# k's layout for the scores: rows laid by 0/1 matmuls in place of copies through DRAM, with q and k turned together on VectorE

## The reference, cut to what matters

```python
# x: [1, 4096, 256], 16 heads of 16, float32
q = (x @ Wq.T + bq).reshape(B, S, H, hd).transpose(0, 2, 1, 3)
k = (x @ Wk.T + bk).reshape(B, S, H, hd).transpose(0, 2, 1, 3)
v = (x @ Wv.T + bv).reshape(B, S, H, hd).transpose(0, 2, 1, 3)
q, k = _apply_rope(q, cos, sin), _apply_rope(k, cos, sin)   # (xr, xi) -> (xr c - xi s, xr s + xi c)
scores = softmax(einsum('bhqd,bhkd->bhqk', q, k) / sqrt(256))
x = _layernorm(x + (scores @ v -> [B, S, D]) @ Wo.T)
x = _layernorm(x + ffn(x))    # gated, two gelu layers of 1024, out to 256
```

## Time and profile before

| | before |
|---|---|
| three runs | 3526.78 us (median), 3524.37 to 3530.44 |
| the profiled execution | 3524.76 us, its span 3523.1 us |
| TensorE busy / weight loads | 3384.9 us (96%) / 1536.3 us |
| VectorE busy | 2987.0 us (85%) |
| ScalarE busy | 2451.1 us (70%) |
| Pool busy | 184.7 us (5%) |
| mean granted clock of TensorE | 0.971 |

### The profile page before, as it was taken

How to read it: one execution, slowest core, us unless ns; L and a number is a source line. 1 busy time by engine, 2 the same in 40 slices (tenths; PEclk the granted TensorE clock), 3 DMA queues, 4 the chain that set the end, 5 groups by cost and what they waited for, 6 DMA issues and landing times. The chain is left out here.

```text
span 3523.1 us, 67331 instructions
## 1 busy us (share of the span) xinstructions
PE 3384.9 (96%) x27994; PEld 1536.3 (44%) x27994; DVE 2987.0 (85%) x3188; ACT 2451.1 (70%) x4472; POOL 184.7 (5%) x320
## 2 busy tenths in 40 slices
PE   8569999999999999999999999999999699999998
PEld 3223333333333333333333333333333278888887
DVE  6599999999999999999999999999996045555554
ACT  2108888888888888888888888888889622222222
POOL 3300000000000000000000000000000000000000
PEclk9759999999999999999999999999999899999999
DMA  8920000000000010001000000000000220000000
GB/s 212 219 42 6 20 12 12 24 12 12 12 24 16 15 60 14 12 11 61 11 12 30 14 12 12 12 12 12 12 8 5 92 96 25 25 25 26 25 13 13
DMA packets 60037, 113.78 MB, mean 32 GB/s; under 512 B 11719, under 2 KB 23624, under 8 KB 59560
## 3 DMA queue, kind: packets, MB, share of 16 engines
q1 hardware_dynamic: 53048, 93.83, 9.7%
q0 software_dynamic: 6688, 15.68, 1.5%
HBM read 82.20 MB, written 37.22 MB: 34 GB/s over the span
## 5 line engine op out<-in xcount | busy, mean ns | idle before, releaser
L710 DVE TENSOR_REDUCE group_max<-wide 128x2 f32<-128x1024 f32 x2048 | 2473.0, 1223 | 22.5 <-PE wide L521 15.8
L681 ACT ACTIVATE probs<-scores 128x512 f32<-128x512 f32 x4046 | 2202.9, 600 | 290.1 <-PE scores L606 42.0
L547 PE MATMUL sums<-probs,v_all 128*17 128x256 f32 (+1 forms) x16120 | 1277.2, 389 | 7.7 <-ACT mixed L664 6.8
L606 PE MATMUL scores<-q_sb,k_all 51*128 51x512 f32 x3968 | 988.5, 495 | 6.7 <-ACT probs L681 5.7
L521 PE MATMUL wide<-k_all,q_sb 48*128 48x512 f32 x4096 | 850.1, 411 | 52.9 <-DVE group_max L710 26.7
L606 PEld LDWEIGHTS scores<-q_sb,k_all 51*128 51x128 f32 x3968 | 370.6, 183 | 842.9 <-ACT probs L681 829.4
L547 PEld LDWEIGHTS sums<-probs,v_all 128*17 128x17 f32 x16120 | 267.1, 95 | 747.4 <-issue 364.9
L521 PEld LDWEIGHTS wide<-k_all,q_sb 48*128 48x128 f32 x4096 | 397.6, 190 | 91.5 <-DVE group_max L710 63.9
L1073 ACT ACTIVATE whole_hid<-acc,scale 128x512 f32<-128x512 f32 x128 | 84.7, 689 | 297.5 <-PE acc L954 297.3
L954 PE MATMUL acc<-hid_b,h2T 128*128 128x512 f32 x1024 | 241.6, 397 | 0.0
L954 PE MATMUL acc<-hid_a,h1T 128*128 128x512 f32 x1024 | 240.2, 394 | 0.0
(11 more groups left out here) (88 smaller groups left out, 1171.1 us busy)
## 6 DMA issues: line engine op xcount, KB each, us to landing
k_all<-k_parts SPq DMA_DIRECT2D x96, 128.0 KB, 5.2
q_sb<-q_parts SPq DMA_DIRECT2D x192, 64.0 KB, 2.5
q_parts<-parts SPq DMA_DIRECT2D x16, 512.0 KB, 6.0
k_parts<-parts SPq DMA_DIRECT2D x16, 512.0 KB, 6.3
heads<-mixed SPq DMA_DIRECT2D x128, 34.0 KB
xt<-in_xT SPq DMA_DIRECT2D x8, 512.0 KB, 6.3
w_words<-in_h1T POOLq DMA_DIRECT2D x32, 128.0 KB, 2.4
w_words<-in_h2T POOLq DMA_DIRECT2D x32, 128.0 KB, 2.3
```

Source lines behind the costliest of these rows:

```text
L547: last = pe.matmul(sums[32 * j:32 * j + HD + 1, cols], v_all[:, g, kt, j], probs[(kt * HG + j) % RING][:, cols], start=(kt == 0 and cols.s ...
L606: pe.matmul(scores[(s + e) % BANKS][:], k_all[rows, g * GP + j, n // HG * P:(n // HG + 1) * P], q_sb[g][rows, j], start=True, stop=True).t ...
L681: act.activation(probs[n % RING][:], bank, ACT.Exp, scale=INV_SCALE)\
L710: dve.reduce_max(group_max[:, n], wide[n % 2][:], AX_X).then_inc(wide_free, 1)
```

## The change

k is not stored in DRAM any more. q and k of one half of features form one item of 1024 columns, so there are 16 items in place of 32: VectorE's shuffle, multiplications, addition, rounding and subtraction each take both together, and VectorE multiplies by the sines too. For k's part of an item, TensorE runs eight matmuls in fp32r (`spread_k`): on each of four row tiles of 32 rows (two heads) a 0/1 matrix picks the high part for its two places in both halves, and a second one the low part for its place, summed into one bank per row tile. ScalarE copies the four banks into `k_all`, adding a column that is 1 in the rows of ones and 0 elsewhere. q's and k's projections have one bank each, in place of four in turn; the order of the work on TensorE is written out: q and k of the first half, v, the spread of the previous chunk's second half, q and k of the second half, the spread of the first half. v's bias is added by one fp32r matmul over all rows (bias high part in one row, low part in another) in place of the float32 one of a single row. `v_all` has its token tiles outermost, so ScalarE copies two tiles of v at once. One of the two `parts` buffers lies in the last columns of `k_all`, which are written last. The loops are written out rather than run as hardware loops. In `attend` the last placement, the rows of ones and the waits for them are gone. The core of the diff:

```diff
-def place_k(sp, k_parts, k_all, c, ft, done):
...
@@ project @@
...
+        item = [sb(f"item{b}", [P, 2, CH]) for b in range(2)]
+        pair = sb("pair", [P, 2, CH])
+        lent = k_all[:, JP:, (NCH - 1) * CH:].rearrange("p (a t) s -> p a t s", a=2)
+        parts = [lent, sb("parts", [P, 2, 2, CH], F32R)[:]]
...
+        ps = [psum(f"ps_{t}", [P, CH]) for t in "qk"]
...
+        spread = [psum(f"ps_spread{j}", [P, CH]) for j in range(JP)]
...
-                place_k(sp, parts_dram[1], k_all, c, ft, k_in)
...
+            for c in range(NCH):
+                for ft in range(FT):
+                    i = c * FT + ft
+                    sp.wait_ge(low_done, i + 1)
+                    dst = q_dram.rearrange("a f s -> f a s")[ft * P:(ft + 1) * P]
+                    sp.dma_start(dst[:, :, c * CH:(c + 1) * CH], parts[i % 2][:, :, 0].bitcast(F32)).then_inc(q_stored[i % 2], 16)
+                if c + 2 < NCH:
+                    sp.wait_ge(v_ready, 2 * c + 2)
+                    sp.wait_ge(projected, (c + 1) * 2 * FT)
+                    sp.wait_ge(rotated, (c + 1) * FT)
+                    load(c + 2)
...
-                        pool.tensor_tensor(pair[m % 2][:], pair[m % 2][:], table[p][:, 1], ALU.mult).then_inc(sine_done, 1)
...
         def _(pe):
+            def item_of(c, ft):
+                n = c * FT + ft
+                for t in range(2):
+                    if n == 0:
+                        pe.wait_ge(w_in[t], 16)
+                    else:
+                        pe.wait_ge(biased, 2 * (n - 1) + t + 1)
                     for i in range(FT):
+                        last = pe.matmul(ps[t][:], w_sb[:, t, i, ft * P:(ft + 1) * P], xt[c % 2][:, i],
                                          start=(i == 0), stop=(i == FT - 1))
                     last.then_inc(projected, 1)
+            def values(c):
+                if c == 0:
+                    pe.wait_ge(v_weights_in, 48)
+                    pe.wait_ge(bv_set, 3)
                 for a in range(2):
+                    if c > 0:
+                        pe.wait_ge(v_free, (c - 1) * 2 + a + 1)
                     for b in range(2):
                         tt = 2 * a + b
                         for i in range(FT):
+                            pe.matmul(psv[a][:, b], xt[c % 2][:, i, tt * P:(tt + 1) * P], wv_sb[:, i],
                                       start=(i == 0), stop=False)
+                        last = pe.matmul(psv[a][:, b], two_rows[:], bv_parts[:], start=False, stop=True)
                     last.then_inc(v_ready, 1)
+            def spread_k(c, ft):
+                i = c * FT + ft
+                if i == 0:
+                    pe.wait_ge(choose_set, 5)
+                pe.wait_ge(low_done, i + 1)
+                if i > 0:
+                    pe.wait_ge(spread_free, JP * i)
+                for a in range(2):
+                    for j in range(JP):
+                        rows = slice(j * ROWS, (j + 1) * ROWS)
+                        last = pe.matmul(spread[j][:], choose[rows, a], parts[i % 2][rows, a, 1],
+                                         start=(a == 0), stop=(a == 1))
+                        if a == 1:
+                            last.then_inc(spread_ready, 1)
+            for c in range(NCH):
+                pe.wait_ge(x_in[c % 2], (c // 2 + 1) * 16)
+                item_of(c, 0)
+                values(c)
+                if c > 0:
+                    spread_k(c - 1, 1)
+                item_of(c, 1)
+                spread_k(c, 0)
+            spread_k(NCH - 1, 1)
         def _(act):
+            def bias(c, ft):
+                n = c * FT + ft
+                if n == 1:
+                    act.wait_ge(bv_set, 3)
+                if n >= 2:
+                    act.wait_ge(low_done, n - 1)
+                for t in range(2):
+                    act.wait_ge(projected, 2 * n + t + 1)
+                    act.activation(item[n % 2][:, t], ps[t][:], ACT.Identity, bias=b_sb[:, t, ft:ft + 1]).then_inc(biased, 1)
+            def values(c):
+                for a in range(2):
+                    act.wait_ge(v_ready, c * 2 + a + 1)
+                    at = c * TT + 2 * a
+                    dst = v_all[:, at:at + 2, :, :, 0:HD].rearrange("p a g j d -> p a (g j) d")
+                    act.activation(dst, psv[a][:].rearrange("p a (h d) -> p a h d", d=HD), ACT.Copy).then_inc(v_free, 1)
+            def spread_k(c, ft):
+                i = c * FT + ft
+                if i == NCH * FT - 1:
+                    act.wait_ge(q_stored[0], 16 * NCH * FT // 2)
+                for j in range(JP):
+                    act.wait_ge(spread_ready, i * JP + j + 1)
+                    act.activation(k_all[:, ft * JP + j, c * CH:(c + 1) * CH], spread[j][:], ACT.Identity,
+                                   bias=ones_rows[:]).then_inc(spread_free, 1)
...
         def _(dve):
+            def swap(n):
+                dve.wait_ge(biased, 2 * n + 2)
+                if n > 0:
+                    dve.wait_ge(rotated, n)
+                dve.stream_shuffle(pair[:].rearrange("p t s -> p (t s)"), item[n % 2][:].rearrange("p t s -> p (t s)"),
+                                   [q ^ 1 for q in range(32)]).then_inc(swapped, 1)
+            def rotate(n):
+                c = n // FT
+                cos, sin = [table[c % 2][:, a].unsqueeze(1).to_broadcast([P, 2, CH]) for a in range(2)]
+                dve.wait_ge(swapped, n + 1)
+                dve.tensor_tensor(item[n % 2][:], item[n % 2][:], cos, ALU.mult).then_inc(cosine_done, 1)
+                dve.tensor_tensor(pair[:], pair[:], sin, ALU.mult).then_inc(sine_done, 1)
+                dve.wait_ge(cosine_done, n + 1)
+                dve.wait_ge(sine_done, n + 1)
+                dve.tensor_tensor(item[n % 2][:], item[n % 2][:], pair[:], ALU.add).then_inc(rotated, 1)
+            def high(n):
+                dve.wait_ge(rotated, n + 1)
+                if n >= 2:
+                    dve.wait_ge(q_stored[n % 2], 16 * (n // 2))
+                    dve.wait_ge(spread_ready, JP * (n - 1))
+                dve.tensor_copy(parts[n % 2][:, 0], item[n % 2][:]).then_inc(high_done, 1)
+            def low(n):
+                dve.wait_ge(high_done, n + 1)
+                dve.tensor_tensor(parts[n % 2][:, 1], item[n % 2][:], parts[n % 2][:, 0].bitcast(F32), ALU.subtract)                    .then_inc(low_done, 1)
...
+            for n in range(TOTAL):
+                if n % FT == 0:
+                    dve.wait_ge(table_in[n // FT % 2], (n // FT // 2 + 1) * 32)
+                swap(n)
+                if n > 0:
+                    low(n - 1)
+                rotate(n)
+                high(n)
+            low(TOTAL - 1)
@@ attend @@
...
-            place_k(sp, k_parts, k_all, NCH - 1, FT - 1, k_in)
...
-            sp.wait_ge(ones_set, 1)
...
-                sp.dma_start(rows.bitcast(F32), src).then_inc(k_ones, 16)
...
-                    pe.wait_ge(k_in, 16 * PLACES)
...
+                    last = pe.matmul(sums[32 * j:32 * j + HD + 1, cols], v_all[:, kt, g, j],
...
-            pe.wait_ge(k_ones, 16 * PAIR)
```

More of the change, by code:

```diff
@@ L58 @@
 SLOT = SHIFT_ROW + 3
-PLACES = PAIR * len(K_PART)
-def place_k(sp, k_parts, k_all, c, ft, done):
[L63 to L69, removed]
+PLACES = PAIR * len(Q_PART)
 def place_q(sp, q_parts, q_sb, c, g, done):
@@ L124, in project @@
         low_done = sem("low_done")
-        parts_free = [sem(f"parts_free{b}") for b in range(2)]
-        k_in = sem("k_in")
+        q_stored = [sem(f"q_stored{b}") for b in range(2)]
+        spread_ready = sem("spread_ready")
+        spread_free = sem("spread_free")
         v_ready = sem("v_ready")
         v_free = sem("v_free")
-        waited = sem("project_waited")
-        sp_waited = sem("sp_waited")
+        zeros_set = sem("zeros_set")
         ones_set = sem("ones_set")
[L133 to L138, removed]
+        eye_set = sem("eye_set")
+        choose_set = sem("choose_set")
+        bv_set = sem("bv_set")
+        bv_sb = item[1][:, 0, 0:D]
+        eye = item[1][:, 1, 0:P]
+        same = item[1][:, 1, P:P + ROWS]
         block = ctx.enter_context(nc.Block())
@@ L163, in chunk @@
[L163 to L173, removed]
+            sp.dma_start(w_sb[:, 0], io["wqT"].rearrange("(t p) o -> p t o", p=P)).then_inc(w_in[0], 16)
+            load(0)
@@ L181, in _ @@
[L181 to L196, removed]
+            for at in (0, ROWS):
+                sp.dma_start(bv_sb[at:at + 1], io["bv"].rearrange("(o d) -> o d", o=1)).then_inc(v_weights_in, 16)
@@ L216, in _ @@
+            pool.memset(eye, 0.0).then_inc(eye_set, 1)
+            pool.memset(choose[:].bitcast(F32), 0.0).then_inc(choose_set, 1)
+            pool.wait_ge(eye_set, 1)
+            pool.affine_select(out=eye, in_=eye, compare_op=ALU.not_equal, fill=1.0, base=0,
+                               pattern=[[-1, P]], channel_multiplier=1).then_inc(eye_set, 1)
+            pool.memset(v_all[:, :, :, :, HD:HD + 1], 1.0).then_inc(ones_set, 1)
```

(28 more changed lines are left out.)

144 lines of the change are left out of this document (30 added, 114 removed).

## The result

| | before | after |
|---|---|---|
| median of 4 runs | 3526.82 us | 3505.19 us (3503.68 to 3506.62) |
| ratio | | 0.9944, 95% interval 0.9931 to 0.9956 |
| profiled execution: its time, its span | 3524.76, 3523.1 us | 3506.62, 3505.0 us |
| first maxima's matmul starts | 179.78 us | 160.84 us |
| from there to the end | 3343.3 us | 3344.2 us |

A forecast was written before the change was run, and what follows sets the result against it. The prediction took DMA transfers to bound the projection; after the change, TensorE's 13.2 us work, 3.4 wait and 2.25 low clock make 18.85 us a chunk against 19.7. Gain 9.4 us: 3526.8 to 3517.4 us, range 3502 to 3527.

The forecast's parts named there:

- rival A: Main forecast: projection chunks of 18.85 us against 19.7, a gain of 9.4 us, 3507 to 3526 us; chance 0.66.
- rival B: TensorE's clock stays up in the projection: chunk 16.6 us, total 3500.8 us; chance 0.09.
- The transfers bound the kernel before, and go: Projection: DMA engines full; without k's stores and placements a chunk's load takes 8.5 us in place of 19.
- The release of x behind the low part: x's load, issued after the second half's low part, takes 6.3 us and is wanted over 9 later: hidden.
- VectorE 6.6 us an item, ScalarE not the bound: Projection: VectorE alone would allow 13.1 us a chunk; ScalarE's 14 operations take 8.6 to 9.7 us.
- The new wait of 3.4 us a chunk, and q, k and v queued behind it: TensorE idles 3.4 us before the first half's spread, waiting for VectorE's low part: round 16.6 us, not 13.1.
- The clock falls in every chunk: After each wait TensorE runs at 1.2 GHz for a mean 4.5 us, losing 2.25 us a chunk.
- TensorE's work, 13.2 us a chunk: At the full clock: q and k 6.9, v 4.7, two spreads 1.6 us.
- C: A spread gains nothing beyond pairs of row tiles: 1.3 us each, 12 us more, 3529 us; chance 0.12.
- D: A spread's eight matmuls run one after another, 2.6 us: 43 us more, 3561 us; chance 0.08.
- lower bound of 0.44: Least time for a spread on TensorE: each set of four matmuls costs one stream of 512 columns, 0.22 us.
- The sum: First spread at 22.3 us, seven chunks to 154.3, attention's first DMA at 164.8, first maxima at 170.4 against 179.8.

The follow-up runs named there:

- noplace: Kernel before the change, with the readings of k back from DRAM left out except the last six: 3528.9 us, including 27.4 us for setting a constant.
- late: Changed kernel with TensorE and ScalarE reordered: each item's projections, half of v, then the spread of the item two before: 3476.6 us, ratio 0.986 to the kernel before.
- fill: Changed kernel with three float32 matmuls, their result overwritten, put into TensorE's wait for the low part in every chunk: 3493.7 us, ratio 0.9904 to the kernel before.
- onerow: Changed kernel with v's bias added as before, by a float32 matmul of one row: 3523.8 us, ratio 0.9991 to the kernel before.
- double: Changed kernel with the eight matmuls of every spread issued twice: 3514.6 us, ratio 0.9963 to the kernel before.
- pool: Changed kernel with the sines multiplied by Pool again: 3506.0 us, ratio 0.995 to the kernel before.
- late_pool: The reordered kernel late, with the sines multiplied by Pool: 3492.0 us, ratio 0.9905 to the kernel before.

## Why the prediction was right in kind and short in size

The mechanism came as forecast, but the gain was more than twice the forecast one, and that the measured 3505.2 lies in the stated range is in part luck: rival A's own range was 3507 to 3526, and the range reached down to 3502 only as a part of rival B was let in, whose condition (the clock stays up) did not come.

- *The transfers bound the kernel before, and go:* right (noplace, and the DMA share of a third). The release of x behind the low part was hidden, as costed.
- *VectorE 6.6 us an item, ScalarE not the bound:* right; 6.7 measured in late.
- *The new wait of 3.4 us a chunk, and q, k and v queued behind it:* right, 3.2 us idle seven times and more; late shows what it costs.
- *The clock falls in every chunk:* right here, and its cost is shown by fill; in onerow the same wait left it up in two rounds of seven. The term was 2.25 us a chunk and came to 1.8. Rival B, the clock staying up, did not occur; what it would have been worth is what fill recovers, 12.7 us at the first maxima where B had 16.6.
- *TensorE's work, 13.2 us a chunk:* here is most of the miss. At the full clock it was 15.8 - 3.4 = 12.4. The term that was mis-sized is v: 4.7 forecast, 4.0 measured, which is less than the 4.2 of its lower bound (four times 1.06 and no bias). I priced the new bias matmul (0.12, in truth 0.31) and left the four records beside it at 1.06, but they fell to 0.67: with a matmul of one row between them they had paid for it too. q and k were 7.1 in place of 6.9. The spreads were 0.67 in place of 0.8; four row tiles beat two, rivals C and D fell, as did the lower bound of 0.44. The Trainium skill's rule for four row tiles (TensorE: Matmul & The Clock Gate, Packing small matmuls), by which an estimate gave 0.57, agrees with the step from one set to the next (0.57, in double) and is 0.1 short of a set between other matmuls.
- *The sum:* the chunk was 17.65 in place of 18.85, 0.8 of it work and 0.4 the clock, seven times 8.4 us. The start was 0.8 us earlier (first spread at 21.49, forecast 22.3), the end 0.3 better in all (4.3 in place of 4.9 to the first DMA, 6.0 in place of 5.7 behind it). Together 9.5 us: 160.8 in place of 170.4. The runs' medians differ by 21.6, the profiled executions by 18.1; the rest is how a profiled execution lies among its runs.

That VectorE works without Pool carried nothing by itself here (pool); that it takes q and k together, the written-out loops and the new place of `v_all`'s tiles were not taken apart by any run. The matmul for v's bias, which the title does not name, carried 18.6 of the 21.6 us (onerow), since TensorE had become the bound. Such shares do not add up to the whole: late shows that the order of the work alone is worth more than all of it.

## What to carry to other kernels

When a transfer that bounds a stage is removed, write down the next round engine by engine, in queue order: here an in-order TensorE queue put 3.2 us of waiting and 1.8 us of low clock into each chunk, and moving one call behind other work was worth more than the change itself. Price a matmul by the step from the last of its kind to the next, with its neighbours, not by its own record, and one that is added to others by what it adds. Before giving work to Pool, look for what VectorE does at that moment.

## What the runs showed of the hardware that was not expected

- VectorE's and Pool's two-input multiplications of 1024 columns hardly run at the same time (late_pool): VectorE's takes 3.39 us in place of 1.22, or, once in 15 items, Pool's 4.31 in place of 3.2. Before, only the rounding looked slowed, 1.49 in place of 0.43.
- A float32 matmul of one row costs its neighbours: four records of 256 columns between two of them take 1.06 us, with one only behind them 0.95 (onerow), between fp32r matmuls of all 128 rows 0.67 (the changed kernel), at the same clock.
- Matmuls thrown away make a kernel faster: 2.6 us of them in each wait brought 11.5 us, by the clock alone (fill).
- The same wait of TensorE, 3.2 us, was followed by the low clock in all seven rounds of the changed kernel and in five of seven in onerow; in late one of 2.57 us was (0.62 granted from 34.51 to 39.00).
- Eight fp32r matmuls of 512 columns on four row tiles, with their weights, take 0.67 us, 0.08 each, and two such sets in a row 1.13 (double).
